# Attention and routed experts on one core: plain scatters into two rows a token, tail stages spread over more tiles, final stores issued by ScalarE

## The chip, the core and the metric

The kernel runs on one core of a Trainium2 chip. The core has five engines with a queue each: TensorE (PE; its weight loads PEld overlap the matmuls), VectorE (DVE), ScalarE (ACT), GpSimd (POOL) and SyncE (SP), which here only issues transfers. 16 DMA engines move data between HBM and SBUF. An engine works its own instructions in order; semaphores tie the engines together. The metric is the device time of one execution in microseconds.

## The reference

16 sequences of 512 tokens with 128 values go through one layer. All inputs are float32.

```
x = layernorm(x + attention(x))     # 16 heads of 8; two softmaxes mixed, with and without key 0
x = layernorm(x + ffn(x))
ffn: logits = x @ gate_w.T          # 8 experts, each token takes two of them
     out += wte[:, e:e+1] * ((silu(x @ w1[e].T) * (x @ w3[e].T)) @ w2[e].T)
```

## The kernel before, in words

NB = 16 sequences, L = 512, D = 128, QC = 4 chunks of 128 tokens, E = 8 experts with F = 512.

**Attention.** 64 units (a sequence's heads in four groups) run as a software pipeline over PERIODS. After it each sequence gets its residual sum (`residual`, POOL), its layernorm (`ln_stats`, `ln_moments` on DVE, `inverse_deviation` on POOL, `ln_apply` on DVE, which gives `xn`), and its routing (`route`, six parts on DVE, with small matmuls `xt`, `gl`, `px` on PE, copied out by ACT). SP stores `xn` to `x1_d` (`store_x1`) and fills the same rows of `y_d` with zeros (`zero_y`). POOL copies `xn` twice into `XE` with the token's number beside it (`send_x`) and scatters each token's two copies by expert into `rows_d` (`scatter`, four indirect DMAs for each of two choices).

**Tiles.** The tokens of an expert are worked in 78 tiles: 57 of 256 rows (FULL), then 21 of 128. The tables of the first 45 (FIRST) are made from sequences 0 to 12 (ROUTED = 13) before attention ends, the rest later, when all 16 are routed. SP loads tile t into `XG[t % 6]`. PE transposes it (`tile_in`), ACT copies it (`XGT`), PE makes `tile_up` and `tile_lin`, ACT applies Silu, DVE multiplies (`HH`, L1110), PE makes `tile_down(t-1)`, DVE multiplies with the token's weight (`YO`, L1103, called Y(t) in the prediction), and POOL adds the rows by indirect DMA (L1346) to `x1_d` (even t) or `y_d` (odd t). A tile's add waits until that of t - 2, into the same tensor, has landed. ACT copies the expert's W1 and W3 for the next tile (L731). PE's order in step t is up(t), in(t+1), down(t-1), lin(t); DVE's is the tail work of t, Y(t-1), HH(t).

**Tail work.** What is left of sequences 14 and 15 is threaded between tiles by three tables written by hand: `tail(t)` of DVE, `tail(t)` of POOL, which stands ahead of the scatter of tile t, and TAIL_RING for PE and ACT, with (tile, place).

**Final stage.** For each sequence SP loads x1 and y (`final_load`, buffers X1 and Y0, five deep), PE adds them by two matmuls with the identity into one of four PSUM banks, DVE makes statistics, POOL four small operations, ACT four scaled copies into RES (L766), SP stores (`final_store`). SP's own order is load(b+5), store(b).

## Time and profile before

| | |
|---|---|
| time, median of 3 | 1339.41 us (1336.74 to 1347.7) |
| the profiled execution | 1345.57 us, span 1343.7 |
| PE busy | 1274.6 us, 95% of the span |
| DVE, ACT, POOL busy | 940.4, 830.0, 712.2 us |
| moved | 116.73 MB, 87 GB/s over the span |
| chain that ended last | PE 71%, DVE 20%, the rest below 3% each |

Times are microseconds from the start of the span. Attention runs to about 890, the tiles from 900 to 1292, the final stage from there to the end. In the views a row of the timeline has its start, its length, the engine, the line of the kernel, and in brackets how long the engine had idled before and what ended that.

### The profile page before, as it was taken

To read this page: it belongs to the slowest core of one execution; us is meant where nothing else is said; L and a number is where in the kernel's file an instruction comes from. 1 tells how busy PE (TensorE), PEld (TensorE's weight loads), DVE (VectorE), ACT (ScalarE), POOL (GpSimd) and SP (SyncE) were. 2 spreads that over 40 slices of the span, in tenths; PEclk is the share of its full clock that TensorE was granted. 3 is DMA by queue.
4 is the path that set the end of the run, shared out by engine and by line. 5 is a ranking of instruction groups with operands and counts; after the bars stand their busy time and mean duration, and the time that the engine had idled before them with its cause. 6 is when DMAs were issued, how large, how long until landed. Compare 5 with 4: busy or idle time off the path is not lost.

```text
span 1343.7 us, 22455 instructions
## 1 busy us (share of the span) xinstructions
PE 1274.6 (95%) x7263; PEld 654.0 (49%) x7263; DVE 940.4 (70%) x1591; ACT 830.0 (62%) x1615; POOL 712.2 (53%) x902
## 2 busy tenths in 40 slices
PE   4999999999999999999999999969999999999976
PEld 1233333333333333333333333327999999999952
DVE  7768889899898988988998999934444433333324
ACT  1367767777777777777777777754444444445626
POOL 5123254574554644745745644435787555556546
PEclk9589999999999999999999999979999999999989
DMA  5222222323323232333233233231445333333247
GB/s 144 94 68 73 81 82 78 102 73 105 94 89 97 84 99 81 94 96 95 75 103 105 77 98 115 93 112 26 69 63 95 49 50 50 49 48 42 43 126 259
DMA packets 111394, 116.73 MB, mean 87 GB/s; under 512 B 16688, under 2 KB 90032, under 8 KB 111280
## 3 DMA queue, kind: packets, MB, share of 16 engines
q1 hardware_dynamic: 87472, 97.15, 23.9%
q0 software_dynamic: 23808, 18.14, 9.3%
q8 instruction: 61, 1.00, 0.3%
q14 instruction: 53, 0.43, 0.1%
HBM read 70.34 MB, written 44.83 MB: 86 GB/s over the span
## 4 chain that ended last, share of the span: by engine, by line
PE 71%; DVE 20%; issue 2%; DMA 2%; POOL 2%; SPq 2%; ACT 0%; DVEq 0%; POOLq 0%; ACTq 0%
PE acc_ps L506 13%; DVE rowmax_sb L811 12%; PE mx_ps L483 12%; PE ring_ps L494 11%; PE ring_ps L613 9%; PE mx_ps L587 8%; PE mx_ps L597 8%; DVE TN_sb L820 2%; PE mx_ps L645 1%; PE ring_ps L529 1%; PE ring_ps L523 1%; PE ring_ps L521 1%; PE ring_ps L576 1%; PE ring_ps L545 1%; DVE stats_sb L843 1%
## 5 line engine op out<-in xcount | busy, mean ns | idle before, releaser
L811 DVE TENSOR_REDUCE rowmax_sb<-mx_ps 128x2 f32<-128x1024 f32 x512 | 606.1, 1210 | 90.1 <-PE mx_ps L483 86.1
L662 ACT ACTIVATE probs_sb<-ring_ps 128x512 f32<-128x512 f32 x1024 | 560.5, 598 | 114.5 <-PE ring_ps L494 105.4
L494 PE MATMUL ring_ps<-region_sb 74*128 74x512 bf16 x1024 | 361.5, 388 | 1.5 <-ACT probs_sb L662 1.4
L483 PE MATMUL mx_ps<-region_sb 72*128 72x512 bf16 x1024 | 317.8, 393 | 11.5 <-DVE rowmax_sb L811 8.7
L506 PE MATMUL acc_ps<-probs_sb,values_sb 128*32 128x512 f32 x2048 | 275.0, 610 | 5.4 <-DVE TN_sb L820 5.4
L494 PEld LDWEIGHTS ring_ps<-region_sb 74*128 74x128 bf16 x1024 | 102.4, 101 | 231.5 <-ACT probs_sb L662 134.5
L1165 POOL CAST negmax_parts_sb<-negmax_sb 16x128 bf16<-16x128 f32 x64 | 17.9, 280 | 283.8 <-ACT negmax_sb L668 283.8
L731 ACT ACTIVATE xT_sb<-region_sb 128x512 f32 x78 | 49.1, 630 | 188.1 <-PE mx_ps L597 186.8
L483 PEld LDWEIGHTS mx_ps<-region_sb 72*128 72x128 bf16 x1024 | 97.0, 100 | 131.2 <-DVE rowmax_sb L811 47.5
L1346 POOL DMA_INDIRECT x_d<-probs_sb,values_sb x68 | 106.1, 1561 | 89.6 <-DVE probs_sb L1103 64.8
L1270 POOL DMA_INDIRECT rows_d<-sent_sb,pos_sb x128 | 126.4, 987 | 48.1 <-issue 47.2
L1110 DVE TENSOR_TENSOR probs_sb<-mx_ps,probs_sb 128x1024 f32<-128x1024 f32 (+1 forms) x78 | 84.3, 1080 | 91.5 <-PE mx_ps L597 91.5
L1103 DVE TENSOR_SCALAR probs_sb<-ring_ps,values_sb 128x128 f32<-128x128 f32 x135 | 42.0, 346 | 143.3 <-PE ring_ps L613 143.3
L613 PE MATMUL ring_ps<-region_sb,probs_sb 128*128 x1080 | 137.0, 279 | 3.6 <-DVE probs_sb L1110 3.6
L1346 POOL DMA_INDIRECT y_d<-probs_sb,values_sb x67 | 104.5, 1560 | 65.4 <-DVE probs_sb L1103 54.5
L587 PE MATMUL mx_ps<-k_parts_sb,xT_sb 128*128 128x256 f32 (+1 forms) x624 | 132.2, 355 | 0.5 <-ACT k_parts_sb L736 0.5
L613 PEld LDWEIGHTS ring_ps<-region_sb,probs_sb 128*128 128x128 f32 x1080 | 127.9, 193 | 7.8 <-issue 7.7
L587 PEld LDWEIGHTS mx_ps<-k_parts_sb,xT_sb 128*128 128x128 f32 x624 | 107.9, 192 | 13.7 <-ACT k_parts_sb L736 0.9
L506 PEld LDWEIGHTS acc_ps<-probs_sb,values_sb 128*32 128x32 f32 x2048 | 40.6, 108 | 114.3 <-issue 94.8
L752 ACT ACTIVATE probs_sb<-mx_ps 128x1024 f32<-128x1024 f32 (+1 forms) x78 | 70.4, 903 | 4.6 <-PE mx_ps L587 4.6
L597 PE MATMUL mx_ps<-k_parts_sb,full_q_sb 128*128 128x256 f32 (+1 forms) x312 | 65.4, 353 | 0.0
L597 PE MATMUL mx_ps<-k_parts_sb,full_k_sb 128*128 128x256 f32 (+1 forms) x312 | 65.0, 351 | 0.0
(162 smaller groups left out, 1215.6 us busy)
## 6 DMA issues: line engine op xcount, KB each, us to landing
region_sb<-parts_d SPq DMA_DIRECT2D x384, 96.0 KB
values_sb<-rows_d SPq DMA_DIRECT2D x57, 132.0 KB, 2.2
parts_d<-q_parts_sb SPq DMA_DIRECT2D x16, 384.0 KB, 2.7
parts_d<-k_parts_sb SPq DMA_DIRECT2D x16, 384.0 KB, 2.9
xT_sb<-xT SPq DMA_DIRECT2D x16, 256.0 KB, 3.1
x_sb<-x SPq DMA_DIRECT2D x16, 256.0 KB
x_d<-xn_sb SPq DMA_DIRECT2D x16, 256.0 KB, 3.3
y_d<-padrow_sb SPq DMA_DIRECT2D x16, 256.0 KB, 3.6
```

The source lines that it names most:

```text
L483: last = nc.tensor.matmul(mx_ps[n % 2][:, i, :], QS[b % 2][0:KR, h, P * c:P * (c + 1)], KS[b % 2][0:KR, h, :], start=True, stop=True)
L494: nc.tensor.matmul(bank, KS[b % 2][0:KR + MR, h, P * c:P * (c + 1)], QS[b % 2][0:KR + MR, h, :], start=True, stop=True).then_inc(s_ring_re ...
L506: last = nc.tensor.matmul(acc_ps[VW * j:VW * (j + 1), 0, :], VE[b % 2][:, c, HG * g + j, :], PT[u % 2][:, j, c, :], start=(c == 0), stop=( ...
L587: last = nc.tensor.matmul(up_ps[:, c, 0:n], W1T[t % 2][:, P * c:P * (c + 1)], XGT[t % 2][:, 0:n], start=True, stop=True)
L597: last = nc.tensor.matmul(lin_ps[:, c, 0:n], W3T[t % 2][:, P * c:P * (c + 1)], XGT[t % 2][:, 0:n], start=True, stop=True)
L613: last = nc.tensor.matmul(y_ps[:, at:at + D], HH[t % 2][:, c, P * w:P * (w + 1)], W2[:, bass.ds(expert + c * D, D)], start=(c == 0), stop= ...
L662: nc.scalar.activation(PT[u % 2][:, i // QC, i % QC, :], ring_bank("st", u, i), ACT.Exp, scale=SCALE).then_inc(s_ring_done, 1)
L752: nc.scalar.activation(SG[t % 2][:, :, 0:n], up_ps[:, :, 0:n], ACT.Silu).then_inc(s_silu, 1)
L811: V.tensor_reduce(rowmax[u % 2][:, 2 * k:2 * k + 2], mx_ps[n % 2][:, :, :], axis=AXX, op=ALU.max, negate=True).then_inc(s_mx_done, 1)
L1110: V.tensor_tensor(HH[t % 2][:, :, 0:n], lin_ps[:, :, 0:n], SG[t % 2][:, :, 0:n], ALU.mult)\
L1270: G.indirect_dma_start(rows_d, bass.IndirectOffsetOnAxis(ap=pos[b % 2][:, s, c:c + 1], axis=0), XE[b % 2][:, c, s, :], None).then_inc(s_sc ...
L1346: G.indirect_dma_start((x1_d, y_d)[t % 2], bass.IndirectOffsetOnAxis(ap=XG[t % RING][:, w, D:D + 1].bitcast(i32), axis=0), YO[t % YRING][: ...
```

## The change

- `x1_d` goes. `y_d` has two rows a token (2 NT rows); `dest` numbers the first choice's row in the first half and the second's in the second, so each row is written once. The indirect DMA of a tile no longer adds, and no longer waits for an earlier one. `store_x1` and `zero_y` go, with the waits on them.
- `send_x` multiplies by 0.5, so each copy of a token in `rows_d` holds half its value; the copies of W1 and W3 get a scale of 2 (L731 before), and Y becomes a multiply and add of that half row.
- The final stage loads the two halves of `y_d` and adds them as before.
- The three hand-written tables of the tail are spread: attention's remainder and routing of 14 and 15 over tiles 0 to 23, the later tables to tile 34 (27 before).
- SP starts loading tiles when sequences 0 to 12 are scattered (0 to 13 before).
- ACT issues the final stores, behind its own four copies; SP issues loads alone.

```diff
-            def zero_y(b):
-                sp.dma_start(y_b[b], padrow[:, 0:D].unsqueeze(1).to_broadcast([P, QC, D])).then_inc(s_zeroed, 16)
-
-            def store_x1(b):
-                sp.wait_ge(s_xn, b + 1)
-                sp.dma_start(x1_b[b], xn[:, :, :]).then_inc(s_x1_stored, 16)
...
-            sp.wait_ge(s_scattered, SPARE + SENT * (ROUTED + 1))
+            sp.wait_ge(s_scattered, SPARE + SENT * ROUTED)
...
-            for b in range(FRING):
+                for s, rows in enumerate((Y0, Y1)):
+                    sp.dma_start(rows[b % FRING], y_f[s, b]).then_inc(s_f_in[b % FRING], 16)
+
+            for b in range(NB):
                 final_load(b)
...
-                    nc.scalar.activation(to[t % 2], held[:, bass.ds(expert, F)], ACT.Copy).then_inc(s_w_copied, 1)
+
+                    nc.scalar.activation(to[t % 2], held[:, bass.ds(expert, F)], ACT.Copy, scale=2.0)\
+                      .then_inc(s_w_copied, 1)
...
                 last.then_inc(s_f_norm, 1)
+                act.wait_ge(s_f_norm, b + 1)
+                nc.scalar.dma_start(out_f[b], RES[b % FRING]).then_inc(s_f_stored[b % FRING], 16)
...
-                        last = V.tensor_scalar(YO[(t - 1) % YRING][:, w, :], y_ps[:, at:at + D],
-                                               XG[(t - 1) % RING][:, w, D + 1:D + 2], None, ALU.mult)
+                        row = XG[(t - 1) % RING][:, w, :]
+                        last = V.scalar_tensor_tensor(out=YO[(t - 1) % YRING][:, w, :], in0=y_ps[:, at:at + D],
+                                                      scalar=row[:, D + 1:D + 2], in1=row[:, 0:D],
+                                                      op0=ALU.mult, op1=ALU.add)
...
-                elif t == 3:
+                elif t == 5:
                     residual(b)
-                elif t == 4:
+                elif t in (6, 8):
+                    scatter(b - 1, (t - 6) // 2)
+                elif t == 7:
                     inverse_deviation(b)
-                elif t == 5:
+                elif t == 9:
                     send_x(b)
...
-                    G.indirect_dma_start((x1_d, y_d)[t % 2], bass.IndirectOffsetOnAxis(
+                    G.indirect_dma_start(y_d, bass.IndirectOffsetOnAxis(
                         ap=XG[t % RING][:, w, D:D + 1].bitcast(i32), axis=0), YO[t % YRING][:, w, :], None,
-                        bounds_check=NT - 1, oob_is_err=False, compute_op=ALU.add).then_inc(s_y_out[t % YRING], 16)
+                        bounds_check=2 * NT - 1, oob_is_err=False).then_inc(s_y_out[t % YRING], 16)
```

POOL's queue in the tail, from the residual sum of sequence 15 (ahead of tile 3's scatter) to its inverse deviation, before:

```order
L1229 TENSOR_TENSOR ysum_sb<-attn_out_sb,x_sb 128x512 [waits xn_done,x_plus_bo,ring_done]
L1346 DMA y_d<-probs_sb,values_sb 8192x128 [waits y_scattered1,y_drained]
L1346 DMA y_d<-probs_sb,values_sb 8192x128
L1235 TENSOR_SCALAR rstd_sb<-meanvar_sb 128x4 [waits xn_done,ln_step]
L1237 TENSOR_TENSOR rstd_sb<-rstd_sb,minushalf_sb 128x4 [waits rstd_done]
```

And now, the residual ahead of tile 5's scatter:

```order
L1211 TENSOR_TENSOR ysum_sb<-attn_out_sb,x_sb 128x512 [waits xn_done,x_plus_bo,ring_done]
L1321 DMA y_d<-probs_sb,values_sb 16384x128 [waits y_drained]
L1321 DMA y_d<-probs_sb,values_sb 16384x128
L1252 DMA rows_d<-sent_sb,pos_sb 69632x132 [waits sent_x,route_step]
L1252 DMA rows_d<-sent_sb,pos_sb 69632x132 x3
L1321 DMA y_d<-probs_sb,values_sb 16384x128 [waits y_drained]
L1321 DMA y_d<-probs_sb,values_sb 16384x128
L1217 TENSOR_SCALAR rstd_sb<-meanvar_sb 128x4 [waits xn_done,ln_step]
L1219 TENSOR_TENSOR rstd_sb<-rstd_sb,minushalf_sb 128x4 [waits rstd_done]
```

Four scatters of sequence 14's rows and one more tile's pair now stand between the two.

DVE's queue at the same place, from the statistics of sequence 15 to the application of its layernorm, before (tiles 4 and 5):

```order
L843 BN_STATS stats_sb<-ysum_sb 128x6 [waits residual_sum]
L843 BN_STATS stats_sb<-ysum_sb 128x6 x3
L848 BN_AGGR meanvar_sb<-stats_sb 128x2 [waits ln_step] x4
L1103 TENSOR_SCALAR probs_sb<-ring_ps,values_sb 128x128 [waits y_scattered0,y_ready]
L1103 TENSOR_SCALAR probs_sb<-ring_ps,values_sb 128x128
L1110 TENSOR_TENSOR probs_sb<-mx_ps,probs_sb 128x1024 [waits lin_ready,silu_done]
L857 TENSOR_SCALAR xn_sb<-ysum_sb,meanvar_sb,rstd_sb 128x128 [waits ring_ready,sent_x,x1_stored,rstd_done]
```

And now (tiles 6 to 8):

```order
L822 BN_STATS stats_sb<-ysum_sb 128x6 [waits residual_sum]
L822 BN_STATS stats_sb<-ysum_sb 128x6 x3
L827 BN_AGGR meanvar_sb<-stats_sb 128x2 [waits ln_step] x4
L1084 SCALAR_TENSOR_TENSOR probs_sb<-ring_ps,values_sb 128x128 [waits y_scattered2,y_ready]
L1084 SCALAR_TENSOR_TENSOR probs_sb<-ring_ps,values_sb 128x128
L1092 TENSOR_TENSOR probs_sb<-mx_ps,probs_sb 128x1024 [waits lin_ready,silu_done]
L1084 SCALAR_TENSOR_TENSOR probs_sb<-ring_ps,values_sb 128x128 [waits y_scattered0,y_ready]
L1084 SCALAR_TENSOR_TENSOR probs_sb<-ring_ps,values_sb 128x128
L1092 TENSOR_TENSOR probs_sb<-mx_ps,probs_sb 128x1024 [waits lin_ready,silu_done]
L835 TENSOR_SCALAR xn_sb<-ysum_sb,meanvar_sb,rstd_sb 128x128 [waits sent_x,ring_ready,rstd_done]
```

Two tiles' work instead of one stands between them, and the wait for the store of x1 is gone.

SP's queue in the final stage, once the first five pairs of loads are out, before:

```order
L445 DMA probs_sb<-x_d 128x512 [waits final_sum]
L446 DMA probs_sb<-y_d 128x512
L450 DMA out<-probs_sb 128x512 [waits final_norm]
L445 DMA probs_sb<-x_d 128x512 [waits final_sum]
L446 DMA probs_sb<-y_d 128x512
```

And now, on SP and then on ACT:

```order
L429 DMA probs_sb<-y_d 128x512 [waits final_sum]
L429 DMA probs_sb<-y_d 128x512
```

```order
L743 ACTIVATE probs_sb<-mx_ps,final_shift_sb,final_rstd_sb 128x128 [waits final_stored0,final_rstd]
L743 ACTIVATE probs_sb<-mx_ps,final_shift_sb,final_rstd_sb 128x128 x3
L747 DMA out<-probs_sb 128x512 [waits final_norm]
```

The store has moved from between two pairs of loads on SP to behind the four copies on ACT.

## Rows read from the trace of the kernel before

**Rows 1.** Busy time by stretch: from:to, length, engines, clock, DMA share, GB/s

```profile
60.00:890.00 830.00, 816.96 (x4601) 279.02 (x4599) 729.99 (x1103) 609.51 (x1205) 422.14 (x620) 0.99 0.29 90
...
950.00:1220.00 270.00, 270.00 (x1681) 247.15 (x1680) 104.20 (x222) 121.01 (x201) 171.90 (x124) 1.00 0.41 59
...
1292.00:1343.70 51.70, 33.02 (x64) 12.33 (x64) 18.70 (x128) 24.04 (x64) 27.99 (x65) 0.85 0.69 244
```

**Rows 2.** Waits of SP's queue: us in total, times, longest

```profile
SPq L433 <- DMA rows_d<-sent_sb,pos_sb: 11.1, 1, 11.1
```

**Rows 3.** Timeline around the end of attention and tile 0, PE and ACT

```profile
889.28 1.06 PE L506 MATMUL acc_ps<-probs_sb,values_sb 128*32 128x512 f32 x8
...
890.85 0.61 ACT L731 ACTIVATE full_q_sb<-region_sb 128x512 f32 x1
...
899.82 0.66 PE L576 MATMUL ring_ps<-ident_sb,values_sb 128*128 128x128 f32 x2 [9.47 <-DMA values_sb<-rows_d]
900.58 0.38 ACT L736 ACTIVATE k_parts_sb<-ring_ps 128x256 f32<-128x256 f32 x1 [9.12 <-PE ring_ps L576]
...
901.01 3.78 PE L587 MATMUL mx_ps<-k_parts_sb,xT_sb 128*128 128x256 f32 x8 [0.53 <-ACT k_parts_sb L736]
```

**Rows 4.** Timeline of PE at a short gap within attention

```profile
187.06 0.60 PE L483 MATMUL mx_ps<-region_sb 72*128 72x512 bf16 x2 [1.19 <-DVE rowmax_sb L811]
...
188.27 1.94 PE L506 MATMUL acc_ps<-probs_sb,values_sb 128*32 128x512 f32 x8 [0.39 <-DVE TN_sb L820]
```

**Rows 5.** Timeline of PE in the tiles: down(3), then up and down in the steady stage

```profile
938.65 3.38 PE L613 MATMUL ring_ps<-region_sb,probs_sb 128*128 x16 [1.90 <-DVE probs_sb L1110]
...
951.03 1.89 PE L587 MATMUL mx_ps<-k_parts_sb,xT_sb 128*128 128x256 f32 x8
...
952.98 1.95 PE L613 MATMUL ring_ps<-region_sb,probs_sb 128*128 x16
```

**Rows 6.** Timeline of DVE at tiles 3 to 5

```profile
935.14 0.87 DVE L843 BATCH_NORM_STATS2 stats_sb<-ysum_sb 128x6 f32<-128x128 f32 x4 [4.46 <-POOL ysum_sb L1229]
...
936.80 0.59 DVE L1103 TENSOR_SCALAR probs_sb<-ring_ps,values_sb 128x128 f32<-128x128 f32 x2
937.31 1.21 DVE L1110 TENSOR_TENSOR probs_sb<-mx_ps,probs_sb 128x1024 f32<-128x1024 f32 x1
943.00 1.11 DVE L857 TENSOR_SCALAR xn_sb<-ysum_sb,meanvar_sb,rstd_sb 128x128 f32<-128x128 f32 x4 [4.48 <-POOL rstd_sb L1237]
```

**Rows 7.** Timeline of POOL: tile 3's scatter, the inverse deviation, a row scatter

```profile
938.15 1.55 POOL L1346 DMA_INDIRECT y_d<-probs_sb,values_sb  x1 [3.04 <-DVE probs_sb L1103]
940.00 1.55 POOL L1346 DMA_INDIRECT y_d<-probs_sb,values_sb  x1 [0.30 <-issue]
...
941.92 1.04 POOL L1237 TENSOR_TENSOR rstd_sb<-rstd_sb,minushalf_sb 128x4 f32<-128x4 f32 x1
...
956.76 0.96 POOL L1270 DMA_INDIRECT rows_d<-sent_sb,pos_sb  x1 [0.30 <-issue]
```

**Rows 8.** POOL's DMA queue, 884 to 897 (eight to rows_d), 915 to 922 (two adding)

```profile
q0 software_dynamic: 256, 0.54, 12.1%
...
q0 software_dynamic: 288, 0.13, 20.7%
```

**Rows 9.** POOL's groups by line: busy us, mean ns, idle before

```profile
L1229 POOL TENSOR_TENSOR ysum_sb<-attn_out_sb,x_sb 128x512 f32<-128x512 f32 x16 | 20.9, 1304 | 5.0 <-ACT attn_out_sb L690 5.0
```

**Rows 10.** Timeline of SP's queue in the final stage

```profile
1306.80 0.34 SPq L450 DMA_DIRECT2D out<-probs_sb  x1
1307.19 0.43 SPq L445 DMA_DIRECT2D probs_sb<-x_d  x1
...
1324.20 1.38 SPq L445 DMA_DIRECT2D probs_sb<-x_d  x1
```

**Rows 11.** Timeline of ACT in the final stage, an early and the last sequence

```profile
1310.06 1.50 ACT L766 ACTIVATE probs_sb<-mx_ps,final_shift_sb,final_rstd_sb 128x128 f32<-128x128 f32 x4 [0.40 <-POOL final_shift_sb L1360]
...
1337.32 1.50 ACT L766 ACTIVATE probs_sb<-mx_ps,final_shift_sb,final_rstd_sb 128x128 f32<-128x128 f32 x4 [0.46 <-POOL final_shift_sb L1360]
```

95 lines of the change are left out of this document (34 added, 61 removed).

## Prediction

> **What bounds the kernel now.** I read the busy time by stage first. In the attention stage PE works 816.96 of 830 us and in the tile stage 270.00 of 270 [rows 1]: both are bound by TensorE, so nothing the change does to DVE, POOL or the DMA rings there counts unless it makes PE wait. A full tile takes 34 PE records (8 up, 8 lin, 16 down, 2 transposes); 1681 records in 270 us are 49.4 tiles, 5.46 us each. That leaves three places where PE is not the bound: the hand-over from attention to tiles, tiles 0 to 9, where work on sequences 14 and 15 is threaded between tiles, and the final stage, where PE works 33 of 51.7 us [rows 1]. Then I read the waits of SyncE's queue, and the timeline at each place.
>
> **The hand-over.** In the kernel before, SP loads no tile until the rows of sequence 13 have landed; it waits 11.1 us for them, once [rows 2]. PE's last attention matmul begins at 889.28 and ends at 890.34, its next work is the transpose of tile 0 at 899.82, after 9.47 us of waiting for those rows, and up(0) begins at 901.01 [rows 3]. Tiles before FIRST hold rows of sequences 0 to 12 alone, so the new count (ROUTED, not ROUTED + 1) is reached before SP gets there; no store of xn stands ahead of it either, and the loads are issued before attention ends. Next late is then ACT: its two weight copies end at 891.46, the copy of the transposed tile takes 0.38 (0.10 behind the transpose before) and up(0) followed it by 0.05, so up(0) begins at 892.0. **9.0 us earlier**. up(0) also took 3.78 us against 1.89 for the same eight matmuls in the steady stage [rows 3, 5]: twice, as the lower of TensorE's two levels (1.2 and 2.4 GHz) gives, after the long idle. Now PE still idles about 1.1 us before up(0). After a gap of 1.19 us and another of 0.39 an eight-matmul group took 1.94 us against 1.06 [rows 3, 4], so short gaps cost clock as well. Of the 1.89 us at most 0.88 is then lost again: I take 1.0 as won. Term: **-10.0** (ends -9.0 and -10.9).
>
> **Tiles 0 to 9.** Before, PE waited 1.90 us for HH(4) and down(3) then took 3.38 against 1.95 at the lower clock: 3.3 us lost [rows 5]. The reason is in DVE: it stood 4.46 us for the residual sum of sequence 15 (L843), and only then made Y(3) and HH(4) [rows 6]. The residual was late because POOL was behind with normalise and count_rows. The change puts attn_to_rows one tile later and the residual after scatter(4), with no such arrears ahead. With down(4) at 0: Y(4) ends at 2.60 (1.95 for down and 0.65 for Y's two pieces with their start, 0.59 without) [rows 5, 6]; POOL begins its scatter 0.76 later (937.39 to 938.15) [rows 6, 7]. Here the price of one scatter matters, and the trace has no plain scatter of 512 byte rows with a bounds check. Ends: 1.55 us as the adding one (L1346) and 0.96 as the plain one to rows_d (L1270), each with 0.30 between two [rows 7]. Over the queue an adding scatter sent 144 packets (288 for two), a plain one 32 (256 for eight) [rows 8]; descriptors are what POOL makes, and the new one no longer adds, so I take **0.96 to 0.98**. Then scatter(4) runs 3.37 to 5.63, the residual takes 1.30 [rows 9] to 6.93, DVE needs 3.38 from the start of L843 to the end of HH (935.14 to 938.52) [rows 6], HH(6) ends at 10.35 and down(6) is due at 10.92: no stall. **-3.3**.
>
> But the new table makes a wait of its own. ln_apply(15) stands in DVE's order at tile 8, ahead of Y(7) and HH(8), and needs POOL's inverse_deviation at tile 7. POOL has to do scatter(5), four row scatters (tail 6), scatter(6) and then it. From the same zero: Y(5) ends at 9.22, scatter(5) runs 9.99 to 12.25, the four row scatters at 1.26 each end at 17.3, scatter(6) at 19.85, and the two small operations 1.41 us later (941.55 to 942.96) [rows 7] at 21.3. On DVE ln_apply is 1.11, Y and HH 1.72 (936.80 to 938.52), and PE started 0.13 after HH [rows 5, 6]: down(8) begins at 24.3, due at 4 x 5.46 = 21.84. A stall of 2.4, plus 1.43 for the clock as after the 1.90: **+3.8**. At 1.55 a scatter the same chain gives 0.7 at down(6) and 5.2 at down(8), +7.3 with the clock. What queues behind: Y(7) and all of DVE's tiles, PE behind them, and POOL's next four row scatters; these are made good by tile 12, since Y(t) waits only for scatter(t-3).
>
> **The rest of the tile stage.** Y becomes a multiply and add of 128 elements. No such row exists; between the multiply's 0.30 and twice that it stays hidden, since DVE worked 104.20 of 270 us and Y is needed two tiles later. The copies of W1 and W3 get an immediate scale, send_x becomes a multiply; ACT and POOL have idle time at both places (POOL worked 171.90 of 270, ACT 121.01) [rows 1]. The tables of tiles 45 to 77 are made about seven tiles later, by tile 34 for a use at tile 45: no wait. The 32 transfers of 256 KB that are gone (store_x1, zero_y) lay beside a TensorE-bound stage and DMA engines at 0.29 to 0.41 [rows 1]: **0**. The last scatter is on the path: POOL 0.57 shorter, **-0.6** (ends 0 and -1.2, since a write without a read should not land later).
>
> **The final stage.** Before, SP issues store(b) and, behind it, the loads of b+6. The first store went at 1306.80, and the next load at 1307.19 right after it [rows 10], though that load itself waits only for a sum on PE that precedes two stages of work for the store. With stores on ACT the loads run ahead. What then sets the pace? ACT's four operations take 1.50 and it idled 0.40 for POOL in between, a pace of 1.90 [rows 11]; over the whole stage the mean was 2.137 (the last block ends at 1338.82, the first by 1306.80, when its store goes, 15 blocks earlier) [rows 10, 11], the difference being late loads. New on ACT: wait for its own result 0.03, issue 0.34, gap 0.05 as on SP [rows 10]: 1.50 + 0.42 = 1.92, and with some jitter I take 2.0. Sixteen blocks then end 15 x 0.137 = **-2.0** earlier. Ends: POOL's pace 1.90 gives -3.5; an ACT that also waits for one of SP's load issues (0.43 [rows 10]) each time gives 2.35, +3.2.
> The Trainium skill (DMA: Bandwidth & Descriptors, "Issuing engines are not separate DMA queues") says that a transfer runs on the same 16 engines whoever issues it, so a second issuer saves only the issue time. By that the gain would be 16 x 0.39 = 6 us of SP's time and none on the path. The trace shows otherwise only in so far as a load stood behind a store that itself waited.
>
> **Sum.** -10.0 - 3.3 + 3.8 - 0.6 - 2.0 = **-12.1 us**. The profiled execution took 1345.57 (span 1343.7 and 1.87 around it), so 1333.5 in its terms. It lies 6.2 above the median of 1339.41; against that the forecast is **1327.3 us**, 0.9% less.
>
> **Rivals.**
> 1. *Scatters without add cost POOL 1.55 as before* (0.25). For: the bounds check stays, and it may be the price. Against: the packets. The stall at down(8) is 5.2, with 0.7 before: -12.1 + 3.5 + 0.6 = -8.0, **1331.4**.
> 2. *No new stall, or ACT at POOL's pace* (0.28). For: the chain's slack hangs on 14 POOL steps, each known to some tenths; DVE waits nowhere else. Without the stall -15.9, with the pace too -17.4: **1322 to 1323.5**.
> 3. *ACT and SP get in each other's way at issue* (0.12). For: no ACT issue is in the trace, and the ring can hold an issue up: one took 1.38 [rows 10]. With 2.35 a block the stage is 3.2 longer than before: -6.9, **1332.5**. 
> 4. *Slower* (0.05): every store issue on ACT takes 1.38, as that one load did with full rings. The block is 1.50 + 0.03 + 1.38 + 0.05 = 2.96, the last ends 12.3 later than before, in all -12.1 + 2.0 + 12.3 = +2.2: **1341.6**. It decides from a block of 2.8 on.
> The forecast itself has 0.30. All but the fourth are faster, by 0.5 to 1.3%.
>
> **Range and chances.** Rival 1 and 3 reach 1332.5, 1336.6 together; rival 2 reaches 1322, with the start's better end 1321. Range **1320 to 1337**. Faster or slower by over 1% (about what a measurement of this kernel can tell from no change) begins at 1326.0 and 1352.8. The forecast lies 1.3 above the first, so a third of it and all of rival 2 fall below: 0.10 + 0.28, and a little for the start's better end, 0.40. Slower by over 1% needs several times rival 4's price: 0.04. Within 1%: 0.56.
>
> **What would show it.** In the changed profile: up(0) at 892 on the same clock scale, its duration between 1.9 and 3.8; no wait of SP for rows_d; the indirect scatters at about 1.0 and not 1.55; no PE gap before down(4) or down(6), one of 2 to 5 us before down(8), at the place where DVE waits for POOL's inverse deviation; DVE's wait for the residual under 3; in the final stage ACT blocks 1.9 to 2.1 apart and issues of 0.34 on ACT's queue. Wrong it is if PE loses its time elsewhere in tiles 0 to 12 (another wait on POOL), if the attention stage is more than 1 us longer or shorter, or if the last block of ACT ends later after the first than the 32.05 us of before.

## The result and the profile after

The changed kernel took 1336.20 us in the median of ten executions (1327.13 to 1338.60), the kernel before 1341.81 in ten beside them (1334.81 to 1348.07): a ratio of 0.9946, 95% interval 0.9921 to 0.9971, 5.6 us less. The forecast was 1327.3, with 1320 to 1337 as its range. Five more sets of the same changed kernel, each beside executions of the kernel before, came out as follows. The records name the chip of each set but the first. One execution of the chip 1 set took 1339.16 us at a mean granted clock of 0.938, where the others had 0.971 to 0.979; the ratio and interval leave it out, and so does the median in brackets.

| set | median, changed | median, before | ratio and interval |
|---|---|---|---|
| first | 1336.20 | 1341.81 | 0.9946 (0.9921 to 0.9971) |
| chip 5 | 1319.88 | 1339.90 | 0.9878 (0.9827 to 0.9929) |
| chip 0 | 1321.85 | 1336.80 | 0.9856 (0.9812 to 0.9900) |
| chip 5 | 1322.40 | 1342.06 | 0.9889 (0.9841 to 0.9938) |
| chip 9 | 1336.11 | 1342.33 | 0.9961 (0.9931 to 0.9991) |
| chip 1 | 1322.17 (1319.17) | 1338.47 | 0.9889 (0.9852 to 0.9925) |

The first and the fifth row of values belong together, and so do the four others. The same code is worth 0.4 to 0.5% in two sets and 1.1 to 1.4% in four. Most of what follows is about telling these apart.

The page of the first trace after:

```profile
span 1334.3 us, 22328 instructions
PE 1270.0 (95%) x7263; PEld 651.1 (49%) x7263; DVE 942.3 (71%) x1591; ACT 827.1 (62%) x1615; POOL 662.2 (50%) x902
```

The hand-over, timeline of PE and ACT in that trace (where [rows 3] has the kernel before):

```profile
889.65 1.06 PE L481 MATMUL acc_ps<-probs_sb,values_sb 128*32 128x512 f32 x8
890.67 0.42 PE L551 MATMUL ring_ps<-ident_sb,values_sb 128*128 128x128 f32 x2
...
891.76 0.38 ACT L713 ACTIVATE k_parts_sb<-ring_ps 128x256 f32<-128x256 f32 x1
892.20 1.99 PE L562 MATMUL mx_ps<-k_parts_sb,xT_sb 128*128 128x256 f32 x8 [1.11 <-issue]
```

The transpose of tile 0 follows attention at once, up(0) begins at 892.20 (forecast: 892.0), and its eight matmuls take 1.99 us and not 3.78. Against the 1.89 of the steady stage that is 0.1 more, so hardly any clock is lost over the gap of 1.11.

Groups of instructions by line, POOL, first after, then before (columns: count, busy us, mean ns, idle before):

```profile
L1321 POOL DMA_INDIRECT y_d<-probs_sb,values_sb x135 | 132.3, 980 | 222.4 <-DVE probs_sb L1084 196.1 <-issue 26.2
L1227 POOL TENSOR_SCALAR sent_sb<-xn_sb 128x512 f32<-128x512 f32 x32 | 47.5, 1495 | 14.5 <-DVE xn_sb L835 14.5
```

```profile
L1346 POOL DMA_INDIRECT x_d<-probs_sb,values_sb x68 | 106.1, 1561 | 89.6 <-DVE probs_sb L1103 64.8 <-issue 23.4 <-DMA y_d<-probs_sb,values_sb 1.4
L1245 POOL COPY sent_sb<-xn_sb 128x512 f32<-128x512 f32 x32 | 19.2, 646 | 14.1 <-DVE xn_sb L857 14.1
```

A plain scatter of 128 rows with a bounds check costs POOL 0.98 us, an adding one 1.56; the multiply in send_x costs 1.50 where the copy took 0.65.

**Two things blur the time of one execution, and stage lengths remove one of them.** PE's granted clock is at its lower level, 0.50, from about 30 us on, and rises to 1.00 at a time that differs between executions, whatever the kernel. Windows from 40 to 60 and 60 to 80 us (length, PE busy, then the other engines, granted clock, DMA), first the kernel before, then the changed kernel on chip 5:

```profile
40.00:60.00 20.00, 18.82 (x40) 6.07 (x41) 13.01 (x11) 7.09 (x14) 4.16 (x6) 0.50 0.22 69
60.00:80.00 20.00, 20.00 (x64) 7.04 (x66) 10.09 (x10) 9.95 (x19) 4.17 (x6) 0.53 0.23 71
```

```profile
40.00:60.00 20.00, 18.30 (x53) 5.65 (x54) 15.55 (x14) 10.39 (x20) 4.17 (x6) 0.76 0.26 80
60.00:80.00 20.00, 19.91 (x116) 6.60 (x118) 16.55 (x16) 15.31 (x31) 7.15 (x11) 1.00 0.26 81
```

So I take a mark behind this, the first transpose of xn of the second sequence on PE, and measure from it. It lies at 195.3 to 208.2 us in the twenty traces of this study, in four traces of the kernel before alone at 208.2, 196.9, 205.9 and 197.9. The differences of start times in the timelines then are (mark to up(0); up(0) to the start of the last scatter; that to the first final load; first final load to the end; and all four, mark to end):

| trace | chip | to up(0) | tiles | to load | final | mark to end |
|---|---|---|---|---|---|---|
| before, four traces | 5, 4, 14, and the first | 692.8 to 694.3 | 390.6 to 391.6 | 3.2 | 47.3 to 48.9 | 1135.3 to 1136.5 |
| changed, first trace | not named | 687.2 | 392.9 | 2.3 | 47.0 | 1129.3 |
| changed | 5 | 683.2 | 387.0 | 2.3 | 47.3 | 1119.7 |
| changed | 0 | 683.5 | 388.7 | 2.3 | 47.3 | 1121.7 |
| changed | 5 | 683.2 | 387.0 | 2.3 | 47.3 | 1119.8 |
| changed | 9 | 690.6 | 397.8 | 2.3 | 47.9 | 1138.5 |
| changed | 1 | 683.0 | 387.0 | 2.3 | 47.3 | 1119.5 |

The kernel before holds its 1135.8 to within 0.7. The changed one is 14.1 to 16.3 us shorter in four traces, and these agree with each other stage by stage, but for 1.7 us of the tiles on chip 0 (see experiment 7); the two of the sets at 1336 are longer in attention, where the four others agree to 0.6, and in the tiles. The experiments below are read by these lengths, with the median ratio beside them.

The last stretch needs a warning. What ends every one of the twenty traces is neither ACT's last block nor the last store, which lands 2.0 to 2.1 us after that block in all of them. It is a drain on POOL's queue, a sequencer instruction that follows POOL's last operation, and every engine waits for it. Instructions of the closing line (count, duration in ns min/median/max, start), the kernel before, then the changed kernel on chip 5:

```profile
L72 POOLq DRAIN  x1: 6455/6455/6455, 1337.1 to 1337.1; - x1
```

```profile
L71 POOLq DRAIN  x1: 7603/7603/7603, 1309.8 to 1309.8; - x1
```

The drain lasts 6.46 us in the four traces of the kernel before and 7.60 in the six of the changed kernel, on every chip. It is different again in some of the experiments. So 1.15 us of the final stage and of mark to end belong to it and not to what the stage does. What sets its length, these runs do not tell.

### The profile page after: what moved, and what is told of

The parts are those of the page before. It is cut to its first block, busy times and chain, and to the rows that moved or that the text cites. A ratio compares the mean times of both kernels' runs of the same rounds, so it can differ in the third digit from the quotient of the medians.

```text
span 1334.3 us, 22328 instructions
## 1 busy us (share of the span) xinstructions
PE 1270.0 (95%) x7263; PEld 651.1 (49%) x7263; DVE 942.3 (71%) x1591; ACT 827.1 (62%) x1615; POOL 662.2 (50%) x902
## 3 DMA queue, kind: packets, MB, share of 16 engines
q0 software_dynamic: 8688, 18.14, 4.1%
## 4 chain that ended last, share of the span: by engine, by line
PE 79%; DVE 13%; ACT 3%; issue 2%; SPq 1%; DMA 1%; another core or an unknown queue 1%; ACTq 0%; POOL 0%; DVEq 0%; POOLq 0%
PE acc_ps L481 16%; PE ring_ps L469 14%; PE mx_ps L458 13%; PE ring_ps L588 9%; PE mx_ps L572 9%; PE mx_ps L562 8%; DVE rowmax_sb L790 8%; ACT probs_sb L743 2%; PE ring_ps L504 1%; PE ring_ps L498 1%; PE ring_ps L496 1%; PE ring_ps L511 1%; PE ring_ps L551 1%; PE ring_ps L520 1%; PE ring_ps L489 1%
## 5 line engine op out<-in xcount | busy, mean ns | idle before, releaser
L1321 POOL DMA_INDIRECT y_d<-probs_sb,values_sb x135 | 132.3, 980 | 222.4 <-DVE probs_sb L1084 196.1
L1084 DVE SCALAR_TENSOR_TENSOR probs_sb<-ring_ps,values_sb 128x128 f32<-128x128 f32 x135 | 42.1, 347 | 151.8 <-PE ring_ps L588 135.5
L572 PEld LDWEIGHTS mx_ps<-k_parts_sb,full_q_sb 128*128 128x128 f32 x312 | 52.5, 194 | 4.8
```

The source lines that it names most:

```text
L572: last = nc.tensor.matmul(lin_ps[:, c, 0:n], W3T[t % 2][:, P * c:P * (c + 1)], XGT[t % 2][:, 0:n], start=True, stop=True)
L1321: G.indirect_dma_start(y_d, bass.IndirectOffsetOnAxis(ap=XG[t % RING][:, w, D:D + 1].bitcast(i32), axis=0), YO[t % YRING][:, w, :], None, ...
```

## The experiments

**1. The changed kernel again, five times.** No edit.

> The changed kernel once more, unchanged. In its first trace TensorE's signals came 0.7 to 3 us behind its records in two stretches (943 to 960 and 1019 to 1040 us), beside POOL's row scatters of sequences 14 and 15, and about 4 us of TensorE time and clock were lost there. Theory A, it belongs to the new order of POOL's scatters: the same two stretches show it again, tile stage (900 to 1280) PE idle again 4 us or more. Theory B, it is a chance event of one execution: it is gone or lies elsewhere, and the profiled span is 4 us shorter, about 1330. The ratio to the kernel before stays within 0.992 to 0.997.

> The changed kernel, unchanged, a third time. Its first ten executions had a median of 1336.2, six later ones 1319.9, though the kernel before had 1341.8 and 1339.9 beside them; in the first trace an attention sequence took 52.8 to 54.0 us, in the second 52.6 as in the kernel before. Theory: the first set was disturbed by something outside the kernel; here the sequence takes 52.6 again, from the mark of the second sequence to the end 1119 to 1121 us as in the second set, PE waits 2.3 us before down(8), ratio to before 0.985 to 0.991. Rival: the two levels belong to the kernel and come by chance: 1336 is met again in some of the executions.

> The changed kernel, unchanged, a fourth time, to see whether the level of its first ten executions (1336.2) comes back. If it belongs to the place where the first set ran and not to the kernel: median 1319 to 1325, from the second sequence's mark to the end 1119 to 1122 us. If it comes by chance in the kernel itself, some execution lies over 1333, and a trace with sequences of 52.8 us may appear.

> The changed kernel a fifth time. Three later traces had 1119.7, 1121.7 and 1119.8 from the second sequence's mark to the end, the first 1129.3, with TensorE's signals late by up to 3 us in it. If the first set was slow by where or when it ran: again 1119 to 1122, median 1319 to 1325. If it is met in the kernel by chance, one of four sets being slow, a set at 1333 to 1338 may come up here. Where the mark-to-end time is 1121.7 and not 1119.8, up(9) to up(10) behind the 2.3 us wait ran at the lower clock.

> The changed kernel once more beside the next one. On a chip as those of its three fast sets: mark of the second sequence to the end 1119 to 1122, median 1319 to 1325, ratio 0.985 to 0.990; on one as that of the slow sets: 1129 to 1139, signals of TensorE late and attention sequences of 52.8 us and more, ratio 0.995.

The sets are in the two tables above. What sets the two at 1336 apart is in their traces. Waits between 900 and 1250 us that ended by a signal whose sender the trace does not tell (total us, times, longest), first trace after, then chip 9:

```profile
DVE probs_sb L1084 <- remote: 11.7, 3, 5.9
ACT probs_sb L729 <- remote: 8.2, 4, 2.6
ACT xT_sb L707 <- remote: 6.1, 1, 6.1
```

```profile
ACT xnT_sb L667 <- remote: 7.7, 1, 7.7
ACT probs_sb L729 <- remote: 7.3, 2, 4.7
```

The traces of chips 5, 0, 5 and 1 have no such wait there, nor have those of the kernel before. One place of the first trace after, timeline of PE, ACT and DVE:

```profile
1021.03 1.89 PE L562 MATMUL mx_ps<-k_parts_sb,xT_sb 128*128 128x256 f32 x8
...
1023.25 2.05 PE L588 MATMUL ring_ps<-region_sb,probs_sb 128*128 x16
...
1024.68 1.02 ACT L729 ACTIVATE probs_sb<-mx_ps 128x1024 f32<-128x1024 f32 x1 [1.11 <-remote]
...
1027.05 0.61 DVE L1084 SCALAR_TENSOR_TENSOR probs_sb<-ring_ps,values_sb 128x128 f32<-128x128 f32 x2 [1.91 <-remote]
```

up ends at 1022.92 by its record, and the silu that waits for nothing else by then starts at 1024.68; down ends at 1025.30, and Y starts at 1027.05. In the steady stage both follow PE within 0.1. So what waits on PE gets its signal 1.7 us late here, and up to 3 us elsewhere in that trace (lin ends at 1032.70 and the product that needs it starts at 1035.65). A little later such delays meet, and PE itself stands 2.37 us before a down (1037.02), loses clock as well, and the tile stage is 5.9 us longer than on chip 5. Attention shows it in small: a sequence takes 52.6 us from transpose to transpose in the undisturbed traces, and 52.8 to 54.0 in this one. These two traces also hold some 15,600 semaphore events where those of the four other sets hold 19,100; the lateness itself is in the start times above and does not depend on them. The rival of the second repetition (the level comes by chance within a set) is against the counts: of 28 executions in the four sets at 1320 to 1322, 27 lie under 1331 (one at 1339), of 22 in the two sets at 1336 one does (1327.13). It goes with the set. Chip 9 is named for this one and for the first set of experiment 4, whose trace has the late signals too, but these two ran in one session, and the chip of the first set is not on record: whether it is the chip or the session, and what in it, these runs do not settle. The kernel before was never traced on chip 9. Its 20 executions there had a median of 1342.33, against 1336.5 to 1342.1 elsewhere, so it can lose little by it.

**2. The kernel before again.** No edit; three traces, on chips 5, 4 and 14.

> The kernel before, unchanged, for a second trace of it. From the mark of the second sequence to the end 1134 to 1136 us as in its first trace (1135.5), tile stage 390.9 from up(0) to the last scatter, the wait of 9.47 for the rows and of 1.90 before down(3) again, final stage 48 to 49 us. Only the time ahead of the mark (208.2 in the first trace) may differ by up to 12 us. Ratio 1.000.

> The kernel before beside it. If the run is on a chip on which the two-row kernels are slow, its trace tells whether the kernel before has late signals there too (it has none in its two traces so far, and its times moved by 3 us at most between chips). Expected: mark to end 1135 to 1136.5, tile stage 390.9, no late signal, whichever chip it is.

> The kernel before, one look, for the case that it runs on the chip on which the two-row kernels were slow. If the late signals belong to the chip, its trace has them there (sequences over 52.6, mark to end over 1140); if to the two-row kernels on that chip, its trace is as the three others: 1135 to 1136.5. On another chip it only repeats 1135 to 1136.5.

Ratios 0.9995 (0.9963 to 1.0027) and 1.0004 (0.9973 to 1.0034), the third a single execution of 1335.04 beside one of 1334.08. Mark to end 1135.9, 1136.5 and 1135.3. None of the three fell on chip 9, so the question that the last two were to settle stayed open, but they give the reference for all lengths.

**3. The early start alone.**

```
-            sp.wait_ge(s_scattered, SPARE + SENT * (ROUTED + 1))
+            sp.wait_ge(s_scattered, SPARE + SENT * ROUTED)
```

> The kernel before with SyncE's wait for 13 instead of 14 sequences, and nothing else. Theory of the prediction: up(0) begins at 892 instead of 901, the whole kernel is 9 to 10 us faster than before (ratio 0.9925), if the work of sequences 14 and 15 keeps pace. Rival: the early start only moves the wait, since POOL's normalise, count_rows and scatter of sequence 14 and DVE's route still take their time: the stall at down(3) grows from 1.9 to 5 us or more, or a stall appears at tiles 4 to 8, and only 3 to 6 us are won.

Ratio 0.9921 (0.9889 to 0.9953). Mark to up(0) 683.3 instead of 692.8 to 694.3, tiles 389.0 instead of 390.6 to 391.6, mark to end 1123.5: 12.3 us shorter, the drain at the end being 6.46 in both. The rival (the wait only moves) falls. Timeline of PE behind it:

```profile
919.06 2.05 PE L613 MATMUL ring_ps<-region_sb,probs_sb 128*128 x16 [1.91 <-DVE probs_sb L1110]
...
924.66 0.63 PE L541 MATMUL ring_ps<-ident_sb,xn_sb 128*128 128x128 f32 x4 [1.83 <-DVE xn_sb L857]
```

(The group that [rows 5], the prediction and the expectations call down(3) is down(4): down(0) of the kernel before starts at 912.68, the fifth group is the one at 938.65, and it is down(4) that needs HH(4). It is called down(4) from here on.)

The stall before down(4) is as long as before [rows 5], so it does not depend on when the tiles start. But its clock loss does not come, and in its place PE waits 1.83 for the normalised rows of sequence 15. From the start of down(4) to that of down(5) it is 8.86 us here and 8.87 in the kernel before: the slow clock had only filled time in which POOL's inverse deviation was late anyway. The other traces say the same: in all six with this table and the adding scatter it is 10.08 to 10.09 us from up(5) to up(6), though down(4) takes 2.05, 2.73, 2.86, 3.21, 3.38 and 3.68. The clock was no cost of its own there.

**4. The two-row scatter alone**, in the kernel before: late start, old tail table, final stores on SyncE. With the scatter come what it needs: no `store_x1` and `zero_y` and no waits on them, half a row in each copy, the scale of 2, the multiply and add, and two loads of `y_d`.

```
-   G.indirect_dma_start((x1_d, y_d)[t % 2], ..., bounds_check=NT - 1, oob_is_err=False, compute_op=ALU.add)
+   G.indirect_dma_start(y_d, ..., bounds_check=2 * NT - 1, oob_is_err=False)
```

> The kernel before with the two-row plain scatter alone: half the token's row in each, the add by DVE, no stores of xn and no zeroing, two loads of y_d in the final stage; the late start, the old tail table and the stores on SyncE stay. Prediction's reading: the removal of the stall at down(3) belongs to the wide table, so with the old one the 1.9 us stay; tile stage 390 from up(0) to the last scatter, and of this kernel's gain only 0.6 to 1.5 us at the last scatter. Rival, after the pair of old table with either scatter (388.98 adding, 385.18 plain, both with the early start): the cheaper scatter alone frees POOL in time, no stall over 0.5 us at down(3), tile stage 387 (3.8 shorter than 390.8, up(0)'s lost clock kept), mark of the second sequence to the end 1130 to 1132 instead of 1135.7.

> The two-row plain scatter alone in the kernel before, once more, since its first set had TensorE's signals late all through (mark to end 1149.9, attention sequences over 53). If that lateness is tied to the chip it ran on (as the changed kernel's sets at 1336 were) and this set is on another: mark of the second sequence to the end 1130 to 1132, sequence 52.6, tile stage 387, no stall over 0.5 us at down(3), ratio about 0.997. On the same chip: 1350 or more again, with signals late again.

The first set fell on chip 9 and has the late signals too (ratio 1.0063, mark to end 1149.9); the second, on chip 4, does not: ratio 0.9997 (0.9960 to 1.0033), tiles 386.7 instead of 391.1, where the rival had said 387. The final stage is 50.7 instead of 48.2 and mark to end 1133.9, only 1.9 less, because the drain at the end is 8.75 us here and 6.46 in the kernel before; without it mark to end is 4.2 shorter. Timeline of POOL, PE and DVE, the residual sum of sequence 15, then down(4) and what follows:

```profile
923.26 1.29 POOL L1215 TENSOR_TENSOR ysum_sb<-attn_out_sb,x_sb 128x512 f32<-128x512 f32 x1
...
927.60 0.99 POOL L1325 DMA_INDIRECT y_d<-probs_sb,values_sb  x1 [3.06 <-DVE probs_sb L1088]
928.51 1.95 PE L596 MATMUL ring_ps<-region_sb,probs_sb 128*128 x16
...
931.34 1.12 DVE L841 TENSOR_SCALAR xn_sb<-ysum_sb,meanvar_sb,rstd_sb 128x128 f32<-128x128 f32 x4 [3.28 <-POOL rstd_sb L1223]
932.61 0.63 PE L524 MATMUL ring_ps<-ident_sb,xn_sb 128*128 128x128 f32 x4 [0.42 <-DVE xn_sb L841]
```

and the residual sum in the kernel before:

```profile
933.27 1.84 POOL L1229 TENSOR_TENSOR ysum_sb<-attn_out_sb,x_sb 128x512 f32<-128x512 f32 x1
```

down(4) has no gap, with the old table. From up(0) to the end of the residual sum it is 30.5 us here (894.04 to 924.55) and 34.1 in the kernel before (901.01 to 935.11). Six scatters of POOL stand in between, and each is 0.58 cheaper, 3.5 us in all against a difference of 3.6. So the price of the scatter is enough to clear the arrears; the waits that went with it need add nothing.

**5. The old tail table in the changed kernel**, and **6. an adding scatter in it** (both rows zeroed ahead by 32 transfers). Together with experiment 3 they make a square of table and scatter, all with the early start; its corner of old table and adding scatter is the kernel before in everything else (two tensors, a wait for an earlier scatter, `store_x1`, stores on SyncE), so the square is not quite pure. The core of the two edits, POOL's part of the table and the scatter:

```
-                elif t == 5:
+                elif t == 3:
                     residual(b)
-                elif t in (6, 8):
-                    scatter(b - 1, (t - 6) // 2)
-                elif t == 7:
+                elif t == 4:
                     inverse_deviation(b)
...
-                elif t in (20, 21, 22, 23):
+                elif t in (13, 14, 15, 16):
```

```
-                        bounds_check=2 * NT - 1, oob_is_err=False)
+                        bounds_check=2 * NT - 1, oob_is_err=False, compute_op=ALU.add)
```

> The changed kernel with the tail table of before (residual at tile 3, inverse deviation 4, send_x 5, row scatters of 14 at tiles 6 to 9 in halves, of 15 at 13 to 16). Theory: a PE gap of 2 to 5 us before down(3) or down(4), where DVE waits for the residual, as before; none before down(8); in all 1 to 4 us slower than the changed kernel. Rival: the wide table does nothing, since the scatters now cost POOL 0.98 and the arrears are gone by themselves: no gap over 1 us, same time as the changed kernel or 1 to 2 us faster, since the new stall at down(8) is gone too.

> The changed kernel with an adding scatter into the two rows a token (both set to zero first, by 32 transfers of 256 KB as before). It prices the add alone: POOL's scatter 1.55 instead of 0.98 and 144 instead of 32 packets for 128 rows, if the add and not the bounds check is what costs; 0.98 if it was the reading of a third tensor. By the prediction's chain a scatter of 1.55 gives a wait of 0.7 at down(6) and of 5.1 at down(8) instead of 2.3, and the last scatter ends 0.6 later: 3.5 to 5.5 us slower than the changed kernel, about 1.5 of it in clock if at all. Rival: POOL has slack and the time stays within 1 us.

| tiles, up(0) to last scatter | scatter 1.56 | scatter 0.98 |
|---|---|---|
| old table | 389.0 (exp. 3) | 385.2 (exp. 5) |
| wide table | 392.8 (exp. 6) | 387.0, 388.7 (changed) |

Ratios 0.9885 (0.9835 to 0.9936) for 5, 0.9913 (0.9883 to 0.9943) for 6; mark to end 1119.3 and 1123.8. In 5 the theory (a gap where the residual was late) falls and the rival stands: the largest gap of PE in the first tiles is 0.42. The mark-to-end times hide part of the differences, since the drain that ends the kernel is 8.75 us in 5, 5.31 in 6 and 7.60 in the changed kernel; the tile lengths do not have that. The cheaper scatter takes off 3.8 in the old table and 4.2 to 5.8 in the wide one; the wide table costs 1.8 to 3.8 with either scatter. The drains of 5 and of 6:

```profile
L71 POOLq DRAIN  x1: 8747/8747/8747, 1318.3 to 1318.3; - x1
```

```profile
L72 POOLq DRAIN  x1: 5313/5313/5313, 1318.2 to 1318.2; - x1
```

The wide table's cost is where the prediction put it. Timeline of the changed kernel on chip 5, POOL, DVE and PE ahead of down(8):

```profile
930.43 0.97 POOL L1252 DMA_INDIRECT rows_d<-sent_sb,pos_sb  x1 [0.30 <-issue]
931.70 1.00 POOL L1321 DMA_INDIRECT y_d<-probs_sb,values_sb  x1 [0.30 <-issue]
...
934.37 1.04 POOL L1219 TENSOR_TENSOR rstd_sb<-rstd_sb,minushalf_sb 128x4 f32<-128x4 f32 x1
935.45 1.12 DVE L835 TENSOR_SCALAR xn_sb<-ysum_sb,meanvar_sb,rstd_sb 128x128 f32<-128x128 f32 x4 [5.47 <-POOL rstd_sb L1219]
...
938.36 2.05 PE L588 MATMUL ring_ps<-region_sb,probs_sb 128*128 x16 [2.30 <-DVE probs_sb L1092]
```

and of experiment 6, with the adding scatter:

```profile
927.58 2.05 PE L599 MATMUL ring_ps<-region_sb,probs_sb 128*128 x16 [0.54 <-DVE probs_sb L1103]
...
940.89 1.12 DVE L846 TENSOR_SCALAR xn_sb<-ysum_sb,meanvar_sb,rstd_sb 128x128 f32<-128x128 f32 x4 [8.20 <-POOL rstd_sb L1230]
...
943.79 3.78 PE L599 MATMUL ring_ps<-region_sb,probs_sb 128*128 x16 [5.03 <-DVE probs_sb L1103]
```

The chain of POOL steps had given 2.4 at down(8) for a scatter of 0.96 to 0.98, and 0.7 at down(6) and 5.2 at down(8) for one of 1.55; measured are 2.30, 0.54 and 5.03. POOL's scatter takes 1.56 us in 6, with a bounds check in both kernels. The queues agree: POOL's DMA queue over the whole kernel, the changed one and then experiment 6,

```profile
q0 software_dynamic: 8688, 18.14, 4.1%
```

```profile
q0 software_dynamic: 23808, 18.14, 9.4%
```

which for 135 scatters is 112 packets more each, 144 instead of 32. So it is the add that costs, and not the bounds check.

**7. POOL's inverse deviation first.**

```
-                elif t in (6, 8):
-                    scatter(b - 1, (t - 6) // 2)
-                elif t == 7:
-                    inverse_deviation(b)
+                elif t == 6:
+                    inverse_deviation(b)
+                elif t in (7, 8):
+                    scatter(b - 1, t - 7)
```

> The changed kernel with POOL's inverse deviation of sequence 15 at tile 6, ahead of the row scatters of sequence 14, which go to tiles 7 and 8. Theory: the wait before down(8) (2.30 us and 0.1 of clock) comes from those four row scatters standing ahead of it; the wait goes to zero, the tile stage is 2.4 us shorter (384.6 instead of 387.0 from up(0) to the last scatter), ratio to before 0.986. Rival: the four row scatters only delay something else, as Y's scatters at tiles 7 to 9, and a gap of 1 us or more appears at down(9) to down(11).

Ratio 0.9878 (0.9828 to 0.9928). Tiles 384.4, where 384.6 was expected, mark to end 1117.2. PE has no gap over 0.25 us between up(0) and the change to half tiles. Timeline of PE and DVE at tiles 7 and 8:

```profile
937.52 1.10 DVE L835 TENSOR_SCALAR xn_sb<-ysum_sb,meanvar_sb,rstd_sb 128x128 f32<-128x128 f32 x4
...
938.05 1.95 PE L588 MATMUL ring_ps<-region_sb,probs_sb 128*128 x16
...
943.51 1.95 PE L588 MATMUL ring_ps<-region_sb,probs_sb 128*128 x16
```

So the wait belongs to the four row scatters ahead of the inverse deviation, and costs 2.6 us where the clock stays (387.0 against 384.4), 4.2 where it falls (388.7, chip 0).

**8. The final stage.** Three forms: the new one in the kernel before (8a, the lines below added to ACT and the stores taken from SyncE), the old one in the changed kernel (8b, the same lines removed and the stores on SyncE), and experiment 7 with the stores back on SyncE and two more loads ahead of them, so that the loads of b+8 and not of b+6 are the first behind store(b) (8c, run twice). The rows below call the two orders loads six and eight ahead.

```
                 last.then_inc(s_f_norm, 1)
+                act.wait_ge(s_f_norm, b + 1)
+                nc.scalar.dma_start(out_f[b], RES[b % FRING]).then_inc(s_f_stored[b % FRING], 16)
```

and for 8c on SyncE:

```
+            for b in range(FRING + 2):
+                final_load(b)
+            for b in range(NB):
+                if b + FRING + 2 < NB:
+                    final_load(b + FRING + 2)
+                final_store(b)
```

> The kernel before with the final stage of the changed one: stores issued by ACT, SyncE's loads running ahead. Theory: ACT blocks 1.92 us apart instead of 2.14 in the mean, last block 3 us earlier, final stage 1.7 to 2.5 us shorter, ratio 0.998 to 0.9985, at the limit of what five rounds tell. Rival (no gain, since transfers run on the same engines whoever issues them): pace stays at 2.1, ratio 1.000.

> The changed kernel with the final stores back on SyncE's queue, behind the loads, in the order of the kernel before. Theory: the mean pace of ACT's blocks goes from about 2.0 back to 2.14 and the final stage from 47.3 to about 48.7 us, 1.4 to 2 us slower than the changed kernel. Rival (who issues does not matter): 47.3 stays.

> The changed kernel with POOL's inverse deviation ahead of the row scatters, and the final stores on SyncE's queue again, each behind the load of a block eight later instead of six (a load waits for the sum of an earlier block only, which PE has made by then). It tells the issuer from the order: if ACT's issue is what brings the gain, the pace is 2.19 as with stores on SyncE behind the loads of six later, and there is a stall of 3.4 us at block 8; if only the order matters (the transfers run on the same engines whoever issues them), that stall is gone, ACT idles 0.40 between blocks, the pace is 1.91 to 1.95 and the final stage 46 to 47 us. Tile stage 384.4 as with the inverse deviation first. Ratio to before 0.985 to 0.987.

> The changed kernel with POOL's inverse deviation first and the stores on SyncE two blocks further behind the loads, beside the changed kernel on one chip. Mark to end 2.6 to 4.5 us shorter than the changed kernel (1117.2 against 1119.8 to 1121.7 before), no wait at down(8), ratio to before 0.983 to 0.987 on a chip without late signals; if the chip has them, both kernels are slowed by 10 us or more and their order stays.

| | issuer of stores | mean pace of ACT's blocks | final stage | ratio |
|---|---|---|---|---|
| before, four traces | SyncE, loads six ahead | 2.06 to 2.16 | 47.3 to 48.9 | |
| 8a | ACT | 2.04 | 46.9 | 0.9992 (0.9958 to 1.0025) |
| changed, chips 0, 1, 5 | ACT | 1.99 to 2.00 | 47.3 | |
| experiment 7 | ACT | 1.97 | 47.0 | 0.9878 (0.9828 to 0.9928) |
| 8b | SyncE, loads six ahead | 2.19 | 50.7 | 0.9900 (0.9863 to 0.9937) |
| 8c | SyncE, loads eight ahead | 1.95, 1.95 | 47.1, 47.2 | 0.9858 (0.9814 to 0.9902), 0.9863 (0.9815 to 0.9912) |

ACT and SyncE's queue, timeline of the changed kernel on chip 0, then 8b, then 8c:

```profile
1290.35 0.34 ACTq L747 DMA_DIRECT2D out<-probs_sb  x1
1290.74 1.51 ACT L743 ACTIVATE probs_sb<-mx_ps,final_shift_sb,final_rstd_sb 128x128 f32<-128x128 f32 x4 [0.42 <-POOL final_shift_sb L1335]
```

```profile
1298.37 1.90 SPq L429 DMA_DIRECT2D probs_sb<-y_d  x2
1300.32 0.43 SPq L433 DMA_DIRECT2D out<-probs_sb  x1
...
1303.31 1.50 ACT L751 ACTIVATE probs_sb<-mx_ps,final_shift_sb,final_rstd_sb 128x128 f32<-128x128 f32 x4 [3.44 <-POOL final_shift_sb L1341]
```

```profile
1289.27 1.50 ACT L751 ACTIVATE probs_sb<-mx_ps,final_shift_sb,final_rstd_sb 128x128 f32<-128x128 f32 x4 [0.40 <-POOL final_shift_sb L1341]
1290.13 0.43 SPq L433 DMA_DIRECT2D out<-probs_sb  x1
```

With ACT as issuer a block is 1.92 at its shortest (1.51 and an idle time of 0.42, the issue of 0.34 in it), as worked out; that holds for three blocks of this trace, and the eleven behind them are 1.97 to 2.01 apart. With SyncE and loads six ahead the pace between stalls is 1.90, but one stall of 3.44 at block 8 brings the mean to 2.19. PE waits there for the ninth pair of loads, which stands behind a store: it is issued 16.8 us after the first load in 8b, 12.9 in the changed kernel and 13.2 in 8c. With the loads two further ahead the stall is gone, and SyncE as issuer does as well as ACT. So it was the order. By the Trainium skill (DMA: Bandwidth & Descriptors, "Issuing engines are not separate DMA queues") a second issuer saves issue time only, since the transfers share 16 engines; the traces of 8c agree (47.1 and 47.2 with one issuer against 47.0 with two in experiment 7, the rest of the kernel being the same). 8a shows the gain at its smallest: 46.9 us is 0.5 below the shortest of the four traces of the kernel before, and the ratio does not tell it from no change.

Experiment 7 and 8c are the shortest versions, and equal: mark to end 1117.2, and 1117.2 and 1117.3, against 1119.5 to 1121.7 for the changed kernel. The medians do not tell 8c from the changed kernel: 1320.72 against 1319.17 on chip 1, 1322.34 against 1322.40 on chip 5. By lengths both beat the changed kernel; by medians of so few executions they beat only the kernel before.

## Why the prediction was right or wrong, point by point

**The time.** 1336.2 lies 8.9 above the forecast and just inside the range; the gain is 5.6 us where 12.1 were forecast. The sum of -12.1 was not too large: on chips 0, 1 and 5 the same kernel is 14.1 to 16.3 us shorter from the mark to the end, and one of the medians there, 1319.88, even lies below the range. The step that failed for the first set is what the prediction put at nothing: "**The rest of the tile stage.** ... **0**", and attention, which it has no term for. The runs showed in its place 687.2 us to up(0) instead of 683.2 and 392.9 for the tiles instead of 387.0, 9.9 us together, with PE's signals reaching ACT and DVE late. The saved 15 or so minus that is what the first set had. The prediction's own warning, attention over 1 us longer, came in; the cause of the late signals stays open.

**The reference.** The prediction put the 6.2 us between the profiled execution and the median down without a cause. As far as four traces tell it is the start: that execution had its mark at 208.2, the latest of all twenty, and behind the mark the kernel before holds its time to 1.2 us.

The terms, against the four undisturbed traces (means of before: 693.3, 391.1, 3.2, 48.2):

| term | predicted | measured |
|---|---|---|
| up(0) earlier | -9.0 | -9.8 to -10.3; against the first trace alone -9.3 to -9.8 |
| its clock | -1.0 | -2.2 (tiles 391.14 in the mean before, 388.98 in experiment 3) |
| stall at down(4) and its clock | -3.3 | -4.5 (388.98 in experiment 3, 384.44 in experiment 7) |
| new stall at down(8) and its clock | +3.8 | +2.6 in three, +4.2 in one |
| last scatter | -0.6 | -0.9 |
| final stage | -2.0 | -2.1 from its first load to POOL's last operation |
| POOL's drain at the end | none | +1.15 (6.46 to 7.60) |

- **Hand-over.** Right in place and mechanism, experiment 3 shows it alone at -12.3. Mis-sized was the clock: the gap of 1.1 us cost 0.1, where I had taken half of the 1.89 as lost by analogy with [rows 4]; and the matmuls behind up(0) had run slow as well, since from up(0) to up(1) it is 7.7 us now and was 9.4 to 10.4.
- **Stall at down(4).** It is gone, and for another reason than the one given. The step that failed is "The change puts attn_to_rows one tile later and the residual after scatter(4)": experiment 4 has neither, and no stall. The cheaper scatter does it, 3.8 us by experiments 3 and 5. I had priced the scatter only in the new table's chain, never in the old one. This is why a table that I booked at +0.5 costs 1.8 to 3.8. The size of 3.3 is near by luck: 1.43 of it was a clock loss that cost nothing (experiment 3), and the 1.83 us of waiting for the normalised rows, which that loss had hidden, were not in it.
- **Stall at down(8).** Right, 2.30 against 2.4, and 5.03 against 5.2 with the other price. The clock's 1.43 was taken as certain; it came in the two traces on chip 0 (1.6 in the changed kernel) and in none on chips 5, 5 and 1.
- **Scatter at 0.96 to 0.98.** Right, 0.98, and the packets had told it. Rival 1 is refuted as a price, and confirmed as a consequence by experiment 6: tiles 392.8, 4.2 to 5.8 longer than the changed kernel's.
- **The rest of the tiles at nothing.** Right for DVE (347 ns for the multiply-add, 346 for the multiply) and for send_x, though that went from 0.65 to 1.50 us, in the four undisturbed sets. Wrong in the first and the chip 9 set, see above.
- **Last scatter.** POOL's 0.57 and 0.3 of landing.
- **Final stage.** A pace of 2.0 was right, though most blocks are 1.98 and not 1.92 apart, and so was the size of the term. But the prediction counted to ACT's last block, and what ends the kernel is POOL: its drain, a term that the sum does not have, took 1.15 of the 2.1 us back. The four traces of before also have 47.3 to 48.9 for this stage, so a term of 2 us that is worked out from one of them is about as large as their scatter.
- **Rival 2** (no new stall) gave 1322 to 1323.5; four of the six medians are near that, 1319.9 to 1322.4, but not for its reason: the stall is there, and the start's and the scatter's terms were larger. **Rivals 3 and 4** are refuted by issues of 0.34 to 0.38 us on ACT.

## What to carry to other kernels

Compare two kernels stage by stage, from a mark behind the part whose clock varies from execution to execution; here that turned a spread of 11 us between four traces of one kernel into one of 1. Look at what ends the kernel before pricing its last stage: here it was the drain behind POOL's last operation, and not the last store. When an engine's instruction gets cheaper, follow the price through the old schedule first: the stall that a reordering was to remove may be gone by then, and the reordering is left with its cost. An order on an in-order queue decides what a second issuer seems to decide, so try the order alone.

## What the runs showed of the hardware that I had not expected

- One kernel can be 15 us slower in one place than in others, while another that computes the same moves by a few: 1336.11 and 1353.94 (chip 9, one session) against 1319.88 to 1322.40 and 1335.43 for two kernels with the two-row scatter, and 1342.33 against 1336.5 to 1342.1 for the one before. The signals of PE reach ACT and DVE up to 3 us late there. Its cause is open, and so is whether it is the chip or the session.
- A gap of 2.3 us on PE left the clock alone in three traces (the next down took 2.05 us) and lowered it in two (3.44 and 2.71 us, both on chip 0); the gap of 1.9 lowered it in four traces of the kernel before and in 8a (down(4) 2.73 to 3.68) and not in experiment 3 (2.05). A single trace does not give the clock's share of a stall.
- The rise of the clock lies far apart between executions of one kernel on the same data: in the kernel before the granted clock of PE is 0.55 from 70 to 80 us and 1.00 from 80 on in the first trace, and 1.00 from 50 on in that on chip 14. Their marks are 10 us apart.
- POOL's drain behind its last operation takes 5.31, 6.46, 7.60 or 8.75 us, the same to 0.01 in every trace of a kernel, and it ends the kernel. It does not follow the packets of POOL's DMA queue: experiment 5 and the changed kernel both have 8688, and 8.75 and 7.60 us.
